# A residual sum moved from the vector engine to GpSimd, in the last part of a transformer kernel

## The reference, cut to what matters

```python
x = x + _layernorm(_L0_attn_ref(_layernorm(x), ...))
x = x + _layernorm(_L0_ffn_ref(_layernorm(x), ...))
x = x + _layernorm(_L1_attn_ref(_layernorm(x), ...))
x = x + _layernorm(_L1_ffn_ref(_layernorm(x), ...))   # mixture of experts
```

## Time and profile before

| | us |
|---|---|
| median of 3 runs | 3576.29 |
| the 3 runs | 3575.45, 3598.54, 3576.29 |
| span of the profiled execution, first to last instruction | 3535.8 |
| DVE busy in the span | 2704.2 (76%) |
| POOL busy in the span | 1781.8 (50%) |
| PE busy in the span | 3212.6 (91%) |
| final part, from its first DVE instruction to the end of the span | 3435.1 to 3535.8 |

### The profile page before, as it was taken

One profiled execution on the slowest core, in us unless ns is written; L12 is line 12 of the kernel. 1 busy time (PEld: TensorE's weight loads), 2 busy tenths in 40 slices (PEclk: granted clock), 3 DMA queues, 4 the chain that ended last, 5 costly groups with the idle time before them and its releaser, 6 DMA issues. The chain is left out here.

```text
span 3535.8 us, 116953 instructions
## 1 busy us (share of the span) xinstructions
PE 3212.6 (91%) x46878; PEld 2155.6 (61%) x46878; DVE 2704.2 (76%) x5988; ACT 2334.4 (66%) x4989; POOL 1781.8 (50%) x3252
## 2 busy tenths in 40 slices
PE   8989899999999999999999989999779969969960
PEld 6766455555555555555555547888657656648860
DVE  7867899999999999999999954666535437855658
ACT  5555587787788777877887775777534536635533
POOL 1441377777777777777777672111000004646761
PEclk9999899999999999999999999999979989989985
DMA  7697533333333333333333312221051123336667
GB/s 242 222 261 233 90 85 84 79 81 84 82 79 82 84 81 79 83 85 79 80 84 86 75 51 93 79 90 67 25 175 48 48 73 125 116 132 184 190 203 268
DMA packets 380531, 396.76 MB, mean 112 GB/s; under 512 B 121368, under 2 KB 294424, under 8 KB 377816
## 3 DMA queue, kind: packets, MB, share of 16 engines
q1 hardware_dynamic: 366264, 351.46, 35.8%
q0 software_dynamic: 13728, 37.83, 2.9%
HBM read 230.29 MB, written 157.25 MB: 110 GB/s over the span
## 5 line engine op out<-in xcount | busy, mean ns | idle before, releaser
L809 ACT ACTIVATE att_p<-att_st 128x512 f32<-128x512 f32 (+3 forms) x3072 | 1328.4, 492 | 391.8 <-PE att_st L715 360.7
L895 DVE TENSOR_REDUCE att_mcol<-att_ring 128x1 f32<-128x512 f32 (+1 forms) x2048 | 1235.6, 650 | 125.1 <-PE att_ring L715 117.3
L715 PE MATMUL att_st<-att_ops_more 99*32 99x512 bf16 (+3 forms) x9216 | 681.2, 326 | 6.6 <-DMA att_ops_more<-att_mpart 4.8
L715 PE MATMUL att_ring<-att_ops_more 96*32 96x512 bf16 (+3 forms) x9216 | 650.8, 328 | 2.0 <-DMA att_va_more<-values 1.2
L881 POOL TENSOR_SCALAR_AFFINE_SELECT att_p<-att_p 128x512 f32<-128x512 f32 x512 | 324.2, 633 | 378.8 <-ACT att_p L809 369.9
L762 PE MATMUL att_pv<-att_p,att_va_more 128*32 128x512 f32 (+3 forms) x4608 | 475.6, 485 | 4.2 <-POOL att_p L881 2.4
L715 PEld LDWEIGHTS att_st<-att_ops_more 99*32 99x32 bf16 x9216 | 249.0, 97 | 291.5 <-ACT att_p L809 111.3
L715 PE MATMUL att_ring<-c_mask,c_identb 128*32 128x128 bf16 x8192 | 413.9, 221 | 0.0
L715 PEld LDWEIGHTS att_ring<-att_ops_more 96*32 96x32 bf16 x9216 | 252.4, 97 | 133.4 <-issue 40.4
L715 PEld LDWEIGHTS att_ring<-c_mask,c_identb 128*32 128x32 bf16 x8192 | 228.3, 98 | 82.0 <-issue 14.5
L715 PE MATMUL att_st<-att_ops 99*32 99x512 bf16 (+3 forms) x3072 | 229.4, 328 | 8.4 <-DMA att_ops<-att_mpart 8.2
(11 more groups left out here) (298 smaller groups left out, 6663.7 us busy)
## 6 DMA issues: line engine op xcount, KB each, us to landing
att_ops_more<-parts SPq DMA_DIRECT2D x1152, 64.0 KB, 3.0
parts<-prj_pt SPq DMA_DIRECT2D x128, 384.0 KB, 3.2
att_ops<-parts SPq DMA_DIRECT2D x384, 64.0 KB, 2.9
moe_work<-moe_rows SPq DMA_DIRECT2D x79, 261.0 KB
values<-prj_vs SPq DMA_DIRECT2D x16, 1024.0 KB, 6.7
heads<-att_ofin SPq DMA_DIRECT2D x128, 128.0 KB, 2.6
ffn_os<-heads SPq DMA_DIRECT2D x16, 1024.0 KB, 4.9
moe_work<-x SPq DMA_DIRECT2D x32, 512.0 KB, 4.3
```

Source lines behind the costliest of these rows:

```text
L715: ins = nc.tensor.matmul(out[row:row + VC], stationary[:, row:row + VC], moving, start=start, stop=stop, tile_position=(0, row))
L809: act.activation(pr[:, g % R, b, off:GN], stp[(t * NST + n) % NS][:, off:GN], ACT.Exp, scale=SCALE).then_inc(exp_done, 1)
L895: ins = v.tensor_reduce(to[:, h, c, i % HB if c else i:(i % HB if c else i) + 1], of[:, 0:w], AX.X, ALU.max)
```

## The change

The residual sum of the final part, with its three waits, leaves DVE and is issued by POOL, with the same operands and the same buffers. POOL's order becomes: `power.serve` of group 0; then for each g, `power.serve` of g + 1 and after it `finish(g)`. On DVE, `combine(g)` gets a wait for `yn` of group g - 2 (`yn_ready` at g - 1), which protects `ya[:, g % 2]` from being written while ACT reads it; before, that order followed from `finish(g-2)` standing ahead of `combine(g)` on DVE.

```diff
@@ gpsimd
+            def finish(g):
+                pool.wait_ge(yn_ready, g + 1)
+                pool.wait_ge(x_back[g % XR], 16 * (g // XR + 1))
+                if g >= 2:
+                    pool.wait_ge(x_stored[g % 2], 16 * (g // 2))
+                pool.tensor_tensor(xo[:, g % 2], xr[:, g % XR], yn[:], ALU.add).then_inc(out_ready, 1)
+
+            power.serve(nc, pool, var[:], rstd[:, 0], G)
             for g in range(G):
-                power.serve(nc, pool, var[:], rstd[:, g % 2], G + g)
+                if g + 1 < G:
+                    power.serve(nc, pool, var[:], rstd[:, (g + 1) % 2], G + g + 1)
+                finish(g)
@@ vector
             def combine(g):
                 r = g % 2
                 v.wait_ge(y_loaded[g % YB], 16 * (g // YB + 1))
+                if g >= 2:
+                    v.wait_ge(yn_ready, g - 1)
                 for k in range(2):
                     own.link(v.tensor_tensor(ya[:, r], yg[:, g % YB, :, k], ya[:, r] if k else sh[:, g], ALU.add))
...
-            def finish(g):
-                v.wait_ge(yn_ready, g + 1)
-                v.wait_ge(x_back[g % XR], 16 * (g // XR + 1))
-                if g >= 2:
-                    v.wait_ge(x_stored[g % 2], 16 * (g // 2))
-                v.tensor_tensor(xo[:, g % 2], xr[:, g % XR], yn[:], ALU.add).then_inc(out_ready, 1)
...
                 if g + 1 < G:
                     out_var(g + 1)
-                finish(g)
```

## The result

The kernel after takes 3597.48 us (median of 20 runs), the kernel before 3581.18 us (20 runs): a ratio of 1.005, 95% interval 1.0036 to 1.0063, so 13 to 23 us slower. The ratios in this text are taken over all the runs; they are not quotients of the two medians. The forecast was +15.7 us on 3576.3.

A forecast was written before the change was run, and what follows sets the result against it. The order of work on DVE was taken to set the pace. 14 periods at +0.90 us (+12.7) and +3.0 us at the end gave +15.7 us on the 3576.3 us median: 3592 us, range 3578 to 3601.

The forecast's parts named there:

- Relief of DVE: 4.81 us without contention: Final part: without the 1.14 us residual sum on DVE, the 5.956 us period would be 4.81 us.
- POOL's sum: 2.31 us: Quiet duration of the 128x1024 residual sum on POOL, extrapolated at 2.05 ns an element from 240- and 512-element operations.
- the lower bound of 1.6 us: Lowest price of POOL's sum, from a 128x256 operation with one operand broadcast (0.616 us); the time would be 3581.
- Exclusion, B 2.05 us late: Sum B, combine's second 128x1024 sum, waits for POOL's SBUF-reading sum; B's end and the scales come 2.05 us late.
- the small DVE row: Earlier-trace evidence for exclusion: a 128x16 DVE sum took 1.27 us under a POOL operation; 8 elements take 0.168 us.
- POOL gets in ahead of B: POOL's sum starts at 0.90 us, waits for sum A, and runs before sum B; other orders give the same period.
- Period 6.86 us: Final part, between sums A: 4.81 plus 2.05 us, +0.90 us over 5.956, x14 = +12.7 us.
- The end: +3.0 us: Last group, from last variance to end of last residual sum: 5.04 us before, +3.0 us after.
- DMA at nothing: The load of g + 6 and the store, behind POOL's later sum, cost nothing, with loads five groups ahead.
- Sum: +15.7 us: Whole span: +12.7 us from 14 periods and +3.0 us at the end; 3592 us, 0.44% slower.
- about 1% is what a measurement can tell here: About 1% (36 us) was taken as what a measurement of this kernel can tell from no change.
- 40.5 us lie between the span and the time of an execution: The median of the runs was put 40.5 us above the profiled span of 3535.8 us.

The follow-up runs named there:

- Experiment 1: Kernel after, with POOL's residual sum replaced by a fill of the output buffer with zeros, which only writes SBUF: period 4.89 us, final part 91.29 us.
- experiment 3: Kernel after, with POOL's sum covering two of four tokens (128x512 instead of 128x1024): period 5.83 us, POOL's sum 1.26 us alone.
- experiments 1 to 3: Experiment 1, experiment 3 and, between them, the kernel after with one operand of sum B from PSUM: period 5.69 us, final part 101.17 us.
- experiment 7: Kernel before, unchanged, profiled once more: time 3599.27 us, span 3597.2 us, final part 100.74 us, period 5.96 us.
- experiment 4: Kernel after, with two yn buffers and POOL's sum released by the next group's scales: 3587.57 us, ratio 0.9982 to the kernel before; final part 91.85 us.

## Why the prediction was right

Step by step, with the trace of the kernel after:

- **Relief of DVE: 4.81 us without contention.** Experiment 1 shows 4.89 us, and so does the second period of the kernel after, which has no POOL sum in it (4.89 us). The mis-sized term is the hand-over: A starts 0.11 us after ACT's end (3512.73 to 3512.84), where the residual sum started 0.02 us after it.
- **POOL's sum: 2.31 us.** 2.34 us. The slope from 240 to 512 elements carried to 1024. At 512 elements the sum takes 1.26 us (experiment 3), as a like operation does in the earlier trace rows. How the lower bound of 1.6 us follows from the row that it names is not told, and no sum of 1024 elements came near it.
- **Exclusion, B 2.05 us late.** 2.02 us (1.22 to 3.24), shown by experiments 1 to 3 to come from B's second SBUF operand against a POOL operation that reads, and to follow the length of POOL's instruction. That the small DVE row weighs as much as the large ones is what made the step safe: sharing of bandwidth would not weigh like that.
- **POOL gets in ahead of B, and the price would not hang on that.** It did, 14 times. In the last group the scales were held instead, for 2.1 us (2.30 instead of 0.16).
- **Period 6.86 us.** 6.91: the 0.08 too little above, 0.03 too much in the hold.
- **The end: +3.0 us.** From the last variance to the end of the last sum 8.16 us instead of 5.04, +3.1. Not forecast: from there to the end of the span it took 4.45 instead of 3.37 us. One microsecond of it is in the closing wait of the program (`SPq L1775 <- PEq L1775`), 1.2 instead of 0.2 us, in all eight profiles of kernels in which POOL writes the output last, and not in the two of the kernel before. What POOL does in it stays open.
- **DMA at nothing.** Right: no DVE wait for a load but the first, DMA share 0.89 in the middle.
- **Sum: +15.7 us.** The final part says +17.5 us. It adds up as 118.23 - 100.69: 11.33 to the last sum A, 2.02 for its sum B, 3.12 for the last group, 1.08 at the end. The medians say +16.3, the interval +13 to +23. The forecast counted 14 periods of +0.90, 12.7 us; measured are 13.35 (11.33 + 2.02), for the same 14 holds. The time itself came out 5.5 us above the 3592 forecast, and 4.9 us of that are the kernel before, whose median of 3 runs was 3576.29 and of 20 runs 3581.18.

Wrong were two sentences beside the sum. One is that about 1% is what a measurement can tell here: twenty runs of each kernel told 0.5% from nothing. The other is that 40.5 us lie between the span and the time of an execution, as start and end. It is about 2 us (experiment 7; 3603.16 and 3601.0 in the kernel after). The rest was the difference between an early execution and the median. It did no harm, since the sum was made as a difference and added to the median.

The rule of the Trainium skill, page "SBUF — State Buffer", section "SBUF: two separate sides", holds for the sum of 1024 elements, which no run had shown when the prediction was made: B was held to 0.13 us before POOL's end (3510.43 less its own 1.22, against 3509.34) and did not run on at a lower rate. For POOL's power it does not hold word for word: the power started at 3505.73 and ran 1.02 us, A started at 3505.93 and still took 1.22 us. Whatever the power holds, it had given it back by then. The measurement decides: the hold is not always the whole instruction. A hold that lasts as long as the reading would fit both cases; no run here tests that.

## What to carry to other kernels

Work moved from DVE to GpSimd is not free time for DVE if it reads SBUF while DVE runs operations with two SBUF operands: here DVE lost 2.0 us in each group to GpSimd's sum, and had saved 1.1. Before moving such work, list DVE's operations in the window where it would run. The `bn_stats` and `bn_aggr` operations, and a sum with one operand in PSUM, lay beside GpSimd's sum at no cost. Those with two SBUF operands paid for what was left of it, however small they were, and so did the variance, a `tensor_scalar` with one. After moving it, look at durations, not at waits: a held operation shows as busy.

## What the runs showed of the hardware beyond that

- A GpSimd fill that only writes SBUF (1.80 us) does not hold a DVE sum with two SBUF operands (1.23 us, experiment 1).
- A DVE `tensor_scalar` with a constant, one SBUF operand, was held to the end of GpSimd's sum (0.69 instead of 0.17 us, experiment 4), while `bn_stats` with one SBUF operand was not (1.40 us for four). One operand is thus not enough for every kind of operation.
- The DMA engines moved 387 GB/s in the middle of experiment 4, where 20 us of the kernel before show 356 and, in experiment 7, 369. So the 356 at a share of 0.99 were not the most that they can move: they are about what the kernel before asked for (2.1 MB in 5.956 us are 353 GB/s).
